# A fused GRU and FitzHugh-Nagumo recurrence: the order of VectorE's queue, of the waits, and one product of the candidate

## The reference, cut to what matters

```
# layer 0, GRU cell, h is 4 x 512
gi = x_t @ W_ih + b_ih ;  gh = h @ W_hh + b_hh          (3 x 512 wide: r, z, n)
r = sigmoid(i_r + h_r) ;  z = sigmoid(i_z + h_z)
n = tanh(i_n + r * h_n)
h = (1 - z) * n + z * h                                  x1_t = x_t + h
# layer 1, Runge-Kutta step of order 4, q and p are 4 x 512, drive is x1_t
for each of 4 stages: i = tanh(q_s) @ coupling.T
    dq = q_s - q_s**3/3 - p_s + drive + i + bias ;  dp = 0.08*(q_s + 0.7 - 0.8*p_s)
q, p = clip(q + DT/6*(dq1+2dq2+2dq3+dq4)), clip(p + DT/6*(...))    x2_t = x1_t + q
```

## Time and profile before

| | us |
|---|---|
| median of 3 runs (3658.0 to 3660.68) | 3659.87 |
| the profiled execution, its own time | 3661.45 |
| its span in the profile | 3659.7 |
| DVE's clip of q (L897, once a step), first to last of 512 | 216.7 to 3519.2 |

### The profile page before, as it was taken

One profiled execution on the slowest core, in us unless ns is written; L12 is line 12 of the kernel. 1 busy time (PEld: TensorE's weight loads), 2 busy tenths in 40 slices (PEclk: granted clock), 3 DMA queues, 4 the chain that ended last, 5 costly groups with the idle time before them and its releaser, 6 DMA issues.

```text
span 3659.7 us, 298613 instructions
## 1 busy us (share of the span) xinstructions
PE 3546.2 (97%) x115469; PEld 3220.4 (88%) x115469; DVE 2998.4 (82%) x20699; ACT 2574.2 (70%) x22689; POOL 1507.0 (41%) x6169
## 2 busy tenths in 40 slices
PE   8989999999999999999999999999999999999978
PEld 4479999999999999999999999999999999999954
DVE  2078888888888888888888888888888888888876
ACT  3257777777777777777777777777777777777753
POOL 0034444444444444444444444444444444444421
PEclk9999999999999999999999999999999999999978
DMA  3000000000000000000000000000000000000001
GB/s 127 23 25 1 1 1 1 1 1 1 1 1 1 1 1 1 1 1 1 1 1 1 1 1 1 1 1 1 1 1 1 1 1 1 1 1 1 1 2 46
DMA packets 9454, 24.45 MB, mean 7 GB/s; under 512 B 557, under 2 KB 601, under 8 KB 8793
## 3 DMA queue, kind: packets, MB, share of 16 engines
q1 hardware_dynamic: 8832, 19.92, 1.5%
q10 hardware_dynamic: 88, 0.02, 0.0%
HBM read 15.75 MB, written 4.19 MB: 5 GB/s over the span
## 4 chain that ended last, share of the span: by engine, by line
PE 79%; DVE 14%; issue 4%; ACT 3%; DVEq 0%; DMA 0%; ACTq 0%; POOL 0%; POOLq 0%
PE psum L1180 43%; PE psum L1138 29%; PE psum L1108 5%; DVE psum L887 2%; DVE tpart L843 2%; DVE gates L776 2%; ACT tpart L571 1%; PE psum L1283 1%; DVE psum L878 1%; DVE psum L866 1%; DVE fresh L795 1%; DVE narg L787 1%; DVE hs L812 1%; ACT tfull L573 1%; DVE hpart L819 0%
## 5 line engine op out<-in xcount | busy, mean ns | idle before, releaser
L1180 PE MATMUL psum<-tpart,cpl 128*128 128x32 f16 x65536 | 1995.8, 177 | 34.1 <-DVE tpart L843 15.0
L1180 PEld LDWEIGHTS psum<-tpart,cpl 128*128 128x128 f16 x65536 | 1788.7, 96 | 150.9 <-DVE tpart L843 41.5
L1138 PE MATMUL psum<-hpart,whh 128*128 128x32 f16 x49152 | 1622.9, 176 | 28.8 <-DVE hpart L819 24.4
L1138 PEld LDWEIGHTS psum<-hpart,whh 128*128 128x128 f16 x49152 | 1404.1, 96 | 91.5 <-DVE hpart L819 30.4
L843 DVE SCALAR_TENSOR_TENSOR tpart<-tfull,tpart 128x8 f16<-128x8 f32 x4096 | 668.4, 163 | 146.6 <-ACT tfull L573 9.9
L571 ACT ACTIVATE tpart<-psum 128x8 f16<-128x8 f32 x3072 | 544.0, 177 | 245.8 <-DVE psum L887 177.2
L887 DVE TENSOR_REDUCE psum<-psum 128x8 f32<-128x24 f32 x3072 | 585.5, 192 | 133.9 <-PE psum L1180 12.2
L573 ACT ACTIVATE tfull<-psum 128x8 f32<-128x8 f32 x3072 | 529.2, 172 | 0.0
L571 ACT ACTIVATE tpart<-qnext 128x8 f16<-128x8 f32 x1024 | 213.9, 209 | 434.6 <-DVE qnext L887 434.5
L535 ACT ACTIVATE qterm<-psum 128x16 f32<-128x16 f32 x3072 | 400.6, 184 | 111.0 <-DVE psum L866 109.1
L374 POOL TENSOR_TENSOR kept<-rz,hs 128x8 f32<-128x8 f32 x1024 | 209.2, 204 | 466.5 <-ACT rz L500 465.6
(11 more groups left out here) (152 smaller groups left out, 4040.5 us busy)
## 6 DMA issues: line engine op xcount, KB each, us to landing
xrow<-in_x_dram SPq DMA_DIRECT2D x4, 1024.0 KB, 11.3
out_dram<-space SPq DMA_DIRECT2D x16, 256.0 KB, 2.0
wih<-in_L_cond_W_ih_dram SPq DMA_DIRECT2D x3, 1024.0 KB, 9.6
space<-in_L_cond_W_hh_dram SPq DMA_DIRECT2D x1, 3072.0 KB, 18.6
space<-in_L_cond_coupling_dram SPq DMA_DIRECT2D x1, 1024.0 KB, 19.2
xrow<-in_cond_dram SPq DMA_DIRECT2D x1, 1024.0 KB, 4.7
wih<-in_L_cond_Wk_dram SPq DMA_DIRECT2D x1, 1024.0 KB, 5.6
wih<-in_L_cond_Wo_dram SPq DMA_DIRECT2D x1, 1024.0 KB, 8.0
```

Of the source, the lines that this page charges most:

```text
L1138: mm = pe.matmul(gate_out[x][:, :, :, c * B:(c + 1) * B], whh[:, w, k, n * P:(n + 1) * P], copies_in(hpart[:, k, :, :]), start=(c == 0 and ...
L1180: mm = pe.matmul(stage_out[a][:, :, :, col:col + B], cpl[:, w, k, n * P:(n + 1) * P], copies_in(tpart[:, s % 2, k, :, :]), start=(col == 0 ...
```

## The change

Every operation of the loop stays, in number and shape, except for one new operation on ACT per half: `scaled_omz` multiplies (1 - z) by the power of two that scales h, so that `weigh` becomes a plain product of two tensors. The low part of tanh becomes a plain subtraction too. The order changes in four places: on DVE `base(2)` goes ahead of `sum_gates(1)`, and behind the third stage the order becomes `cubic(3)`, `weigh(1)`, `base(3)`, `new_high(1)`, `new_h_full(1)`; on ACT `candidate(1)` goes behind the square; on POOL `keep_part(1)` goes from behind the first `sums` update to behind the second. The low part of half b (`h_low(1)`) keeps its place behind the first sum of the fourth stage. Waits are reordered so that the one that is written first, and so belongs to the instruction, is another one than before, and a few waits that others already cover are dropped.

```diff
...
@@ -353,8 +355,8 @@
 
             def first_drive(v):
 
+                pool.wait_ge(phat_ready, v)
                 pool.wait_ge(uhat_ready, v)
-                pool.wait_ge(phat_ready, v)
                 pool.tensor_tensor(drive0[:, :], uhat[:, :], phat[:, :], ALU.subtract).then_inc(drive0_ready, 1)
 
             def new_x(t):
@@ -406,7 +408,7 @@
                     if s == 1 and tail <= T:
                         next_x1(tail, now)
                         next_uhat(tail)
-                    if s == 1 and gru <= T:
+                    if s == 2 and gru <= T:
                         keep_part(1, gru)
 
                 if tail <= T:
@@ -480,6 +482,8 @@
                 act.reg_load(r, kap[0:1, n:n + 1].bitcast(i32))
             k_unh = act.alloc_register("act_scale_h")
             act.reg_load(k_unh, inv[0:1, 0:1].bitcast(i32))
+            k_h = act.alloc_register("act_scale_up")
+            act.reg_load(k_h, scale[0:1, 2:3].bitcast(i32))
             k_minus = act.alloc_register("act_scale_minus")
             act.reg_load(k_minus, kap[0:1, 5:6].bitcast(i32))
             k_c = act.alloc_register("act_scale_c")
@@ -500,6 +504,11 @@
                 act.activation(rz[:, x, :], gates[:, x, HC:HG], ACT.Sigmoid, scale=k_gate).then_inc(rz_ready[x], 1)
                 act.activation(omz[:, x, :], gates[:, x, 2 * HC:HG], ACT.Sigmoid, scale=k_minus).then_inc(omz_ready[x], 1)
 
+            def scaled_omz(x, v):
+
+                act.wait_ge(omz_ready[x], v)
+                act.activation(omzs[:, x, :], omz[:, x, :], ACT.Copy, scale=k_h).then_inc(omzs_ready[x], 1)
+
             def candidate(x, v):
 
                 act.wait_ge(narg_ready[x], v)
@@ -507,9 +516,9 @@
 
             def plain_h(v):
 
-                for x in range(HALVES):
-                    act.wait_ge(hs_ready[x], v)
-                if v > 1:
+                act.wait_ge(hs_ready[1], v)
+                act.wait_ge(hs_ready[0], v)
+                if v in (2, 3):
                     act.wait_ge(x1_ready, v - 1)
                 act.activation(h[:, :], hs[:, v % 2, :], ACT.Copy, scale=k_unh).then_inc(h_ready, 1)
 
@@ -517,6 +526,8 @@
                 gate_input(v)
                 sigmoids(0, v)
                 sigmoids(1, v)
+                scaled_omz(0, v)
+                scaled_omz(1, v)
                 candidate(0, v)
                 candidate(1, v)
                 plain_h(v)
@@ -574,10 +585,10 @@
                                        scale=k_stage[s]).then_inc(tanh_ready[s][a], 1)
                         if s == 1 and a == 0 and gru <= T:
                             candidate(0, gru)
+                        if s == 2 and a == 0 and gru <= T:
+                            scaled_omz(1, gru)
                     if s == 2:
                         stage_terms(2)
-                        if gru <= T:
-                            candidate(1, gru)
                     arg, s_next = (in_halves(qnext[:, :]), 0) if s == 3 else (qt, s + 1)
                     if s < 3 or tail <= T:
                         act.activation(in_halves(sq[:, s_next, :]), arg, ACT.Square,
@@ -589,6 +600,8 @@
                             sigmoids(0, gru)
                         act.wait_ge(cub_ready, stage_count(1, now))
                         stage_terms(0)
+                        if gru <= T:
+                            scaled_omz(0, gru)
                         if 3 <= tail <= T:
                             plain_h(tail)
                     if s == 1:
@@ -598,6 +611,8 @@
                         stage_terms(1)
                         if gru <= T:
                             sigmoids(1, gru)
+                    if s == 2 and gru <= T:
+                        candidate(1, gru)
                     if s == 2 and gru < T:
                         gate_input(gru + 1)
                     if s == 3 and tail <= T:
@@ -770,9 +785,9 @@
 
             def sum_gates(x, v):
 
+                dve.wait_ge(gate_mm[x], v)
                 if x == 0:
                     dve.wait_ge(gibase_ready, v)
-                dve.wait_ge(gate_mm[x], v)
                 dve.tensor_reduce(gates[:, x, :], gate3[x].rearrange("p s c -> p c s")[:, 0:HG, :],
                                   AX.X, ALU.add).then_inc(gate_sum[x], 1)
 
@@ -790,15 +805,14 @@
 
             def weigh(x, v):
 
-                dve.wait_ge(omz_ready[x], v)
                 dve.wait_ge(cand_ready[x], v)
-                dve.scalar_tensor_tensor(fresh[:, x, :], omz[:, x, :], s_h, cand[:, x, :],
-                                         ALU.mult, ALU.mult).then_inc(fresh_ready[x], 1)
+                dve.wait_ge(omzs_ready[x], v)
+                dve.tensor_tensor(fresh[:, x, :], omzs[:, x, :], cand[:, x, :], ALU.mult).then_inc(fresh_ready[x], 1)
 
             def new_high(x, v):
 
+                dve.wait_ge(fresh_ready[x], v)
                 dve.wait_ge(kept_ready[x], v)
-                dve.wait_ge(fresh_ready[x], v)
                 if v < T:
                     if x == 0:
                         dve.wait_ge(ka_read, v)
@@ -813,9 +827,9 @@
 
             def h_low(x, v):
 
-                dve.wait_ge(hi_ready[x], v + 1)
                 if v > 0:
                     dve.wait_ge(hs_ready[x], v)
+                dve.wait_ge(hi_ready[x], v + 1)
                 dve.tensor_tensor(part_of(x, 1), in_k(hs_of(x, v)), part_of(x, 0), ALU.subtract).then_inc(h_parts[x], 1)
 
             dve.wait_ge(in_rows, 80)
@@ -840,9 +854,9 @@
             def split_tanh(s, a, v, ready, n):
 
                 dve.wait_ge(ready, n)
-                dve.scalar_tensor_tensor(tpart[:, s % 2, a * HK:(a + 1) * HK, 1, :],
-                                         tfull[:, a * HC:(a + 1) * HC].rearrange("p (k b) -> p k b", b=B), 1.0,
-                                         tpart[:, s % 2, a * HK:(a + 1) * HK, 0, :], ALU.mult, ALU.subtract).then_inc(t_parts[s][a], 1)
+                dve.tensor_tensor(tpart[:, s % 2, a * HK:(a + 1) * HK, 1, :],
+                                  tfull[:, a * HC:(a + 1) * HC].rearrange("p (k b) -> p k b", b=B),
+                                  tpart[:, s % 2, a * HK:(a + 1) * HK, 0, :], ALU.subtract).then_inc(t_parts[s][a], 1)
 
             for a in range(HALVES):
                 split_tanh(0, a, 1, tanh0_ready, a + 1)
@@ -880,10 +894,11 @@
 
             def sum_stage(s, a, v):
 
-                dve.wait_ge(base_ready, stage_count(s, v))
                 dve.wait_ge(stage_mm[s][a], v)
-                if a == 0 and s in (1, 2):
-                    dve.wait_ge(qterm_ready[s], v)
+                if a == 0:
+                    dve.wait_ge(base_ready, stage_count(s, v))
+                    if s in (1, 2):
+                        dve.wait_ge(qterm_ready[s], v)
                 dve.tensor_reduce(qt[:, a, :] if s < 3 else qnext[:, a * HC:(a + 1) * HC],
                                   stage3[a].rearrange("p s c -> p c s")[:, 0:HC, :],
                                   AX.X, ALU.add).then_inc(stage_sum[s][a], 1)
@@ -891,9 +906,6 @@
             def clip(v):
 
                 dve.wait_ge(stage_sum[3][1], v)
-                if v > 1:
-                    dve.wait_ge(q1plain_ready, v - 1)
-                dve.wait_ge(qterm_ready[0], v)
                 dve.scalar_tensor_tensor(q1[:, :], qnext[:, :], clampq[:, 0:1], lowest,
                                          ALU.min, ALU.max).then_inc(q1_ready, 1)
 
@@ -932,8 +944,9 @@
                 if gated_step:
                     new_high(0, gru)
                     new_h_full(0, gru)
+                base(2, now)
+                if gated_step:
                     sum_gates(1, gru)
-                base(2, now)
                 if gru < T:
                     h_low(0, gru)
 
@@ -945,13 +958,12 @@
                     argument(1, gru)
                 split_tanh(3, 0, now, tanh_ready[2][0], now)
                 split_tanh(3, 1, now, tanh_ready[2][1], now)
+                cubic(3, now)
                 if gated_step:
                     weigh(1, gru)
-                cubic(3, now)
+                base(3, now)
                 if gated_step:
                     new_high(1, gru)
-                base(3, now)
-                if gated_step:
                     new_h_full(1, gru)
 
                 sum_stage(3, 0, now)
```

More of the change, by code:

```diff
@@ L118, in build @@
         omz = sb("omz", [P, HALVES, HC])
+        omzs = sb("omzs", [P, HALVES, HC])
         gated = sb("gated", [P, HALVES, HC])
@@ L257, in build @@
         gate_mm, gate_sum, rz_ready, omz_ready = sem_ab("gate_mm"), sem_ab("gate_sum"), sem_ab("rz_ready"), sem_ab("omz_ready")
+        omzs_ready = sem_ab("omzs_ready")
         gated_ready, narg_ready, cand_ready = sem_ab("gated_ready"), sem_ab("narg_ready"), sem_ab("cand_ready")
```

## The result

| | us |
|---|---|
| before, median of 4 runs (3658.0 to 3661.7) | 3660.27 |
| after, median of 4 runs (3535.29 to 3536.48) | 3536.22 |
| ratio after / before, 95% interval | 0.9661 (0.9644 to 0.9678) |
| span of the profiled execution after | 3534.6 |

The change makes the kernel 124 us faster. The forecast was 79 us (3581), and 3536 lies in its range of 3525 to 3638. The granted PE clock is 0.988 of full over the core, before 0.989, so the gain is not the clock's.

The account below looks back on a forecast made before the run. The prediction took a chain of latencies across PE, DVE and ACT as the bound, losing time in stage 3. A 6.25 us step plus 0.06 of gaps gives 6.31, 0.155 less over 510 steps: 79 us, 3581 us, range 3525 to 3638.

Parts of the forecast that it names:

- The price of a wait's place: A late wait costs 0.11 us standing alone, 0.04 inside the instruction; writing it first saves 0.07 each time it decides.
- the rival's mechanism: Slower rival: a wait's place is worth nothing, only the moves act; 31 us slower, 3691 us, chance 0.06.
- What is late next: At sum_stage(0,0), base(0) sets the step by 0.21, its wait standing alone at 0.11: 6.25 instead of 6.33 us.
- half b's chain of 1.27: From stage 3's second row sum through tanh, square, shift and cubic to the end of base(0): 1.27 us, unchanged.
- The rival in which half a sets it: Larger gain: base(0) is not late, PE's chain over half a sets the step; 163 us, 3497 us, chance 0.07.
- The rival of the smaller gain: sum_gates(1) comes later by base(2)'s whole 0.09, new_high(0) not moving or scaled_omz(1) delaying a tanh; 3624 us, chance 0.12.
- The term of half a: Stages 1 and 2: 0.02 us allowed from sum_stage(0,0) on; weigh(0) gains, but base(2) keeps sum_gates(1) and argument(1) in place.
- Contention at argument(1): Moving keep_part(1) lets the POOL operation run earlier; argument(1) takes 0.165 us of queue instead of 0.19, bounds 0.14 and 0.19.
- Stage 3: cubic(3) ahead of weigh(1) clears DVE's queue; the second sum follows PE's end, 6.90 instead of 7.05, gaining 0.15 us.
- the step without gaps: One loop step picked for showing no stray gap: 6.33 us before, forecast 6.25; the average before lay 0.133 above.
- PE's loop end: PE's start of stage 0 comes 0.08 us later every second step, 0.04 on average; forecast as now covered.
- the wandering gaps: Gaps of DVE's queue that wander over the step, 0.09 us on average; two thirds kept, 0.06, bounds 0.02 and 0.09.

Follow-up runs that it names:

- the run that changes one place alone: After kernel with the base's wait written first again in sum_stage(0,0) only: 3503.62 us, ratio 0.9571.
- the kernel with waits alone: Before kernel with the new order of waits and the dropped waits, operations in their old order: 3533.17 us, ratio 0.9652.
- the 93 us: Before kernel with all the new waits except those of sum_stage: 3567.13 us, ratio 0.9747.

## Why the prediction was right, and which terms it mis-sized

**The price of a wait's place: right.** 0.04 inside the instruction and 0.11 alone were read from three rows of before. After shows 0.03 behind PE, 0.03 behind ACT and 0.11 behind base(0), and the run that changes one place alone measured 33 us against 0.07 x 510 = 36. The Trainium skill's rule that a semaphore between VectorE operations costs nothing extra ("VectorE: DVE Perf Modes", section "The DRAIN you can't avoid", from eight copies in a row) would have the sum behind base(0), both VectorE's, start the same with either order of its waits; the run that changes this alone shows 0.04 instead of 0.11, and 3504 us instead of 3536. So on where the waits stand, the measurement decides against it. For the waits on PE and ACT, which that rule does not speak of, the kernel with waits alone is the test: 3533 us where the rival's mechanism would have left 3660.

**What is late next: right.** The second sum of stage 3 comes from PE's end, half b's chain of 1.27 did not change, and base(0) sets the step with 0.11. The rival in which half a sets it falls with the run that gave the base its place back. The rival of the smaller gain falls as well: new_high(0) did move, 0.14 ahead of before.

**The term of half a: mis-sized, and the largest.** The step is "where base(1) and the recovery terms are the late ones, so I allow 0.02 there". At the first sum of stage 1 it measured 0.06, and that is the largest error of the sum: the recovery terms end 0.07 earlier, since half b's sum in stage 0 does not pay for the late base and has its own late wait inside, and ACT then reaches the terms sooner (the last link is argued). sum_gates(1) and argument(1) therefore did not stay; they came 0.06 and 0.07 earlier than forecast. That base(2) takes its place in front of sum_gates(1) was right, and priced by its run at 11 us.

**Contention at argument(1): right in kind, mis-sized.** The forecast took half of the 0.05; all of it went, 0.14 behind argument(1). The run with keep_part(1) back shows 0.05 and 20 us. The exclusive lock of the Trainium skill ("SBUF — State Buffer", section "Who interferes with whom") would hold an operation with two inputs for as long as a GpSimd read lasts. These rows do not show that: beside a POOL operation of 0.25, the DVE operation is 0.04 longer and the next 0.05 later.

**Stage 3: right on where it ends, wrong on what does it.** The forecast of 6.07 for cubic(3), "no longer behind weigh(1)", and of the whole stall's end rested on the order. The waits alone end the stall (0.04 behind PE with the old order), and the old order put back under the new waits costs 4 us. The forecast took the stall in stage 3 to need the new order, and did not ask what the new waits do to the old one. On the forecast's clock cubic(3) came at 5.97, 0.10 early, most of it by what lies ahead.

**The sum.** Against the forecast, new_high(0) came 0.05 earlier (0.04 of it by the term of half a), sum_gates(1) and argument(1) another 0.01 each, and the low part 0.025: together, up to rounding, the 0.10 by which the step without gaps gained more (0.18) than forecast (0.08). The 0.04 of PE's loop end was hidden, as forecast, and the wandering gaps stayed at 0.068 where 0.06 was taken. 0.09 x 510 = 46 us, and 3581 - 46 = 3535.

**The moves are not worth nothing by themselves.** Under the old waits they give 54 us, under the new ones about none (3536 against 3533). Both parts take away the same stall in front of the second sum: the moves clear the queue to 0.10 behind PE, the waits to 0.04. And two moves pull against each other: base(2) in front of sum_gates(1) makes argument(1) the late one ahead of split_tanh(3,0), where in the kernel with waits alone ACT's tanh is; only then does the POOL operation beside argument(1) cost anything, which keep_part(1)'s move gives back. With sum_gates(1) first the kernel is at 3525, and the kernel with waits alone at 3533; stage 3's order (4) and the product (1.5) leave under 3 us for the rest, which is within the error of such sums.

**The wandering gaps.** The average lay 0.133 above the step without gaps and now lies 0.068 above it, but the gaps themselves did not halve: of the 0.133, 0.04 were PE's loop end, and the other 0.09 became 0.07. Where they fall can be read off the traces.
**Left open.** Which of the other waits (weigh, new_high, h_low, sum_gates, the two dropped at the clip) carries how much of the 93 us was not run; nor was split_tanh's plain subtraction by itself. Of the 34 us of sum_stage's waits it is not separated what their order gives and what the four that are dropped give.

## What to carry to other kernels

For an instruction with several waits, ask for each of them separately which comes last in the trace, and write that one first: the same function needs a different order at different places, and a uniform order leaves time behind (33 us here). Price an edit of the order of a queue only after the waits are in place, since both take away the same stall and the second one tried looks worthless. Count the waits that stand alone, too: here there are five a step fewer, and DVE's gaps come by the number of instructions. And charge a wait that now comes late only to what really follows it: here the first sum of the step paid 0.07 for its base, and the second, from which the next stage's terms come, did not.

## What was not expected of the hardware

- The same wait costs 0.03 to 0.04 us inside the instruction and 0.10 to 0.13 as one of its own, for PE, ACT and DVE as the releaser, and taken for every pair at once, with five waits a step dropped, this is worth 126 us of 3660. By itself, for one wait a step, it is 33 us.
- The same edit can be worth nothing or 34 us: sum_stage's waits alone gave 3664, on top of the others 3567 to 3533.
- DVE's stray gaps of about 0.2 us come at a fixed count: 198 of 224 in the after kernel stand at numbers 56 to 71 of each 128 instructions of its queue.
- A POOL addition that starts in the same instant as a DVE operation with two inputs lengthens it from 0.23 to 0.27 and delays the next by 0.05; started 0.55 earlier it costs nothing.
